# The shared expert of the last twelve tiles moved behind the last routed slot

## What is computed

```python
def step(carry, kvq):                     # first layer, token by token
    W, b = carry
    k, v, q = kvq                         # K, V, Q = x @ theta.T
    g = 2.0 / d_h * (W @ k + b - v)
    W = W - LR * jnp.outer(g, k)
    b = b - LR * g
    return ((W, b), W @ q + b)
x = _layernorm(x + attn(x))
# second layer: E = 8 experts of 512 -> 256 -> 512, the best K = 2 of each token
shared = silu(X @ sW1 + sb1) @ sW2 + sb2
activation = jnp.sqrt(softplus(X @ routing_W.T + expert_bias))
combine = weights of the top 2 of activation, 0 elsewhere
hdn = silu(einsum('nd,edh->enh', Xf, rW1) + rb1[:, None, :])
y = einsum('enh,ehd->end', hdn, rW2) + rb2[:, None, :]
x = _layernorm(x + shared + einsum('ne,end->nd', combine, y))
```

## Time and profile before

| | |
|---|---|
| median of 3 runs | 2472.6 us (2462.72 to 2474.06) |
| the profiled execution | 2472.85 us, its span 2471.0 us |
| busy, share of the span | PE 91%, PE weight loads 78%, DVE 61%, ACT 36%, POOL 46% |
| mean granted TensorE clock | 0.965 of full speed |
| chain that ended last | PE 77%, DVE 8%, unknown queue 5%, issue 4%, ACT 3%, DMA 2% |

### The profile page before, as it was taken

The page is one execution under the profiler, slowest core; times in us unless marked ns, Lnnn a source line. Parts: engine busy times, 40 slices in busy tenths (PEclk is TensorE's granted clock), DMA queues, the critical chain, the costliest instruction groups (busy, mean ns, idle before and its releaser), DMA issues.

```text
span 2471.0 us, 40051 instructions
## 1 busy us (share of the span) xinstructions
PE 2249.5 (91%) x13026; PEld 1939.6 (78%) x13026; DVE 1517.3 (61%) x3626; ACT 896.5 (36%) x1951; POOL 1147.9 (46%) x1090
## 2 busy tenths in 40 slices
PE   6999999999999999999999999888588888999980
PEld 5888888888888888888888888777477767888770
DVE  5556655566656776555666666546445334788797
ACT  3333333333333333333333333223444334444440
POOL 1234433344333337544455433753455555567674
PEclk9999999999999999999999999999789999999995
DMA  4111111111111111111111111102533334788798
GB/s 159 35 35 44 43 35 43 43 35 44 43 39 48 35 36 43 43 40 48 35 43 38 41 39 48 35 18 94 183 99 125 116 100 162 249 293 289 250 348 279
DMA packets 101143, 233.29 MB, mean 94 GB/s; under 512 B 18128, under 2 KB 18768, under 8 KB 100176
## 3 DMA queue, kind: packets, MB, share of 16 engines
q1 hardware_dynamic: 72720, 152.48, 18.0%
q0 software_dynamic: 27936, 78.21, 9.8%
q10 hardware_dynamic: 288, 0.04, 0.0%
HBM read 141.22 MB, written 89.53 MB: 93 GB/s over the span
## 4 chain that ended last, share of the span: by engine, by line
PE 77%; DVE 8%; another core or an unknown queue 5%; issue 4%; ACT 3%; DMA 2%; POOL 1%; DVEq 1%; ACTq 0%; SPq 0%; POOLq 0%
PE banks L115 22%; PE banks L117 22%; PE banks L116 21%; PE banks L121 6%; PE banks L713 2%; PE banks L456 1%; PE banks L552 1%; DVE b_small L1624 1%; PE banks L494 1%; DVE b_Y L1071 1%; DVE xc L1071 1%; PE banks L735 1%; DVE W L1068 1%; DVE b_XL L1068 1%
## 5 line engine op out<-in xcount | busy, mean ns | idle before, releaser
L115 PE MATMUL banks<-W 128*128 128x512 f32 (+1 forms) x2040 | 753.4, 369 | 23.1 <-DVE W L1068 20.1
L117 PE MATMUL banks<-W 128*128 128x512 f32 (+1 forms) x2040 | 719.2, 353 | 0.0
L116 PE MATMUL banks<-W 128*128 128x512 f32 (+1 forms) x2040 | 716.9, 351 | 0.0
L115 PEld LDWEIGHTS banks<-W 128*128 128x128 f32 x2040 | 388.7, 191 | 71.8 <-DVE W L1068 10.8
L117 PEld LDWEIGHTS banks<-W 128*128 128x128 f32 x2040 | 387.8, 190 | 55.1
L116 PEld LDWEIGHTS banks<-W 128*128 128x128 f32 x2040 | 389.3, 191 | 46.8
L776 ACT ACTIVATE W<-banks 128x512 fp32r<-128x512 f32 x320 | 191.1, 597 | 523.4 <-DVE banks L1068 226.3
L1674 POOL TENSOR_TENSOR W<-S,W 128x512 fp32r<-128x512 f32 x256 | 327.5, 1306 | 110.9 <-ACT W L776 110.8
L1674 POOL TENSOR_TENSOR X<-X,B 128x1024 f32<-128x1024 f32 x32 | 78.8, 2461 | 602.1 <-DMA X<-in_x 602.1
L776 ACT ACTIVATE W<-S 128x512 fp32r<-128x512 f32 (+1 forms) x288 | 179.8, 650 | 213.0 <-DVE S L1068 200.0
L1810 POOL DMA_INDIRECT ys<-b_Y,IDX x149 | 152.6, 1024 | 136.0 <-DVE b_Y L1068 111.9
(11 more groups left out here) (156 smaller groups left out, 4421.0 us busy)
## 6 DMA issues: line engine op xcount, KB each, us to landing
RG<-ys SPq DMA_DIRECT2D x128, 256.0 KB
XT<-in_xT SPq DMA_DIRECT2D x32, 512.0 KB
X<-in_x SPq DMA_DIRECT2D x32, 512.0 KB, 3.5
x1d<-X SPq DMA_DIRECT2D x64, 256.0 KB
zd<-X SPq DMA_DIRECT2D x64, 256.0 KB, 2.0
b_Y<-zd SPq DMA_DIRECT2D x64, 256.0 KB
out<-b_Y SPq DMA_DIRECT2D x64, 256.0 KB
S<-in_we SPq DMA_DIRECT2D x32, 256.0 KB, 4.8
```

Source lines behind the costliest of these rows:

```text
L115: e.matmul(o, ll, rh, start=start, stop=False, skip_group_check=True)
L116: e.matmul(o, lh, rl, start=False, stop=False, skip_group_check=True)
L117: return e.matmul(o, lh, rh, start=False, stop=stop, skip_group_check=True)
```

## The change

For the last group (tiles 52 to 63, `k.late` = 52) the first stage keeps only the routing logits: `up_x1` multiplies 8 columns, and `back_x1`, `down_x1`, `half_x1`, `residual_x1` and `store_z` return at once on every engine. `load_x` no longer waits for z there. While the last group's later slots run (from the 13th on, a slot can't be of expert 0) the shared expert's four blocks of weights are loaded again into spare Y buffers (iterations 131, 134, 137 and 140, SP), and split by ACT two and by POOL three iterations later into the place of expert 0. Twelve further items run in the slots' pipeline behind slot 148 (M = N + 12): they load a whole tile of `x1d` by SP instead of a gather, use static addresses, and their `down_late` adds the product onto the tile's Y buffer, into which POOL's new `residual` has put tile plus bias. The bases of the finals stay. The last finals' `scale` goes from DVE to ACT, for which POOL's `root` gets two more small operations. The scratch `zd` keeps 52 tiles.

```diff
 def plan_of(k):
-    seq = slots(a) + spread(slots(b), ends(a), 5) + spread(slots(c), ends(b), 5) + ends(c)
+    seq = slots(a) + spread(slots(b), ends(a), 5) + spread(slots(c), ends(b), 5)
+    p.again, p.stage = c["slot"] + c["tiles"], {}
...
+            if (i - p.again) % 3 == 1 and 0 <= i - p.again < 12:
+                q = (i - p.again) // 3
+                x = min(range(RING), key=lambda x: free[x])
+                free[x], p.stage[i] = i + 6, q
...
+    for j, (kind, n, g) in enumerate(ends(c)):
+        base = max(N + j + 1, base + 1)
+        p.finals.append(Final(n, g, base))
...
+    p.M = N + c["tiles"]
 # tensor_program
         for dc in range(KC):
-            z = mm3(e, o[:, 0:LGW], ..., dc == 0, dc == KC - 1)
+            z = mm3(e, o[:, c], ..., dc == 0, dc == KC - 1)   # c = H:LGW for i >= k.late
 def back_x1 / down_x1 (each engine), half_x1, residual_x1, store_z
+        if i >= k.late:
+            return
 def up(i)
+        else:
+            w.wait_ge(k.s_shlo, 7)
...
+                wh, wl = (k.W[:, j * 1024 + dc * H:j * 1024 + (dc + 1) * H] for j in range(2))
-    for i in range(-2, N + 2):
+    for i in range(-2, M + 2):
 # scalar_program
+    def split_again(q):
+        hi, _, raw = again(k, q)
+        w.wait_ge(k.d_sh, 48 + 16 * (q + 1))
+        w.wait_ge(k.s_dn, k.plan.again)
+        copy(hi, raw).then_inc(k.s_shhi, 1)
+    def scale(c):
+        y, i = k.Y[k.plan.buffer["final", c]], c % 2
+        w.wait_ge(k.s_crs, 2 * c + 2 + 2 * (c - k.plan.late + 1))
+        w.wait_ge(k.s_o, c)
+        e.activation(y[:], y[:], ACT.Identity, bias=k.sd2[:, i, 0:1], scale=k.sd2[:, i, 1:2]).then_inc(k.s_o, 1)
 # vector_program
+    def down_late(i):
+        y = k.Y[k.plan.buffer["final", k.plan.late + i - N]]
+        w.wait_ge(k.s_pre, i - N + 1)
+        w.wait_ge(k.s_dn, i + 1)
+        tt(y[:], at["dn", i], y[:], ALU.add).then_inc(k.s_Y, 1)
...
-        if i - 4 in k.plan.base:
+        if k.plan.base.get(i - 4, k.plan.late) < k.plan.late:
             scale(k.plan.base[i - 4])
 # gpsimd_program, load(i) for i >= 3
-            w.wait_ge(k.s_dn1, k.NTL)
+            w.wait_ge(k.s_dn1, k.late)
+            w.wait_ge(k.s_LG, k.NTL)
 # root(c), for c >= late
+            e.tensor_scalar(k.sd2[:, i, 0:1], k.mv2[:, i, 0:1], -1.0, None, ALU.mult).then_inc(k.s_crs, 1)
+            tt(k.sd2[:, i, 0:1], k.sd2[:, i, 0:1], k.sd2[:, i, 1:2], ALU.mult).then_inc(k.s_crs, 1)
+    def residual(i):
+        use = "final", k.plan.late + i - N
+        w.wait_ge(*k.d_tx.of(i - N))
+        w.wait_ge(k.d_sh, 144)
+        tt(k.Y[k.plan.buffer[use]][:], k.XN[i % XNS][:], k.brow[:, 0:D], ALU.add).then_inc(k.s_pre, 1)
+    def split_again(q):
+        tt(lo, raw, f32(hi), ALU.subtract).then_inc(k.s_shlo, 1)
 # sync_program, load_x(t)
-        w.wait_ge(*k.d_z.of(2 * t - 2))
-        w.wait_ge(*k.d_z.of(2 * t - 1))
+        if 2 * t <= k.late:
+            w.wait_ge(*k.d_z.of(2 * t - 2))
+            w.wait_ge(*k.d_z.of(2 * t - 1))
...
+    def load_again(q):
+        e.dma_start(again(k, q)[2], a["we"][E][:, q * D:(q + 1) * D]).then_inc(k.d_sh, 16)
+    def biases_again():
+        e.dma_start(k.brow[:, 0:D], a["b2"][:, E * D:(E + 1) * D].broadcast_to([P, D])).then_inc(k.d_sh, 16)
+        e.dma_start(k.b1T[:, 0:2], a["b1T"][:, 2 * E:2 * E + 2]).then_inc(k.d_sh, 16)
+    def load_late(i):
+        w.wait_ge(k.s_tp, i - XNS + 1)
+        w.wait_ge(k.s_pre, i - XNS - N + 1)
+        e.dma_start(k.XN[i % XNS][:], k.x1d[n * P:(n + 1) * P, :]).then_inc(k.d_tx.sem(i - N), 16)
```

More of the change, by code:

```diff
@@ L384, in plan_of @@
         p.buffer[use], p.before[use], holder[x] = x, holder.get(x), use
-    p.N = len(k.items)
+    p.N = N = len(k.items)
+    p.late = len(p.finals)
+    for j, (kind, n, g) in enumerate(ends(c)):
+        base = max(N + j + 1, base + 1)
+        use = ("final", len(p.finals))
+        p.finals.append(Final(n, g, base))
+        x = min(range(RING), key=lambda x: free[x])
+        assert free[x] <= N + j
+        free[x] = base + 6
+        p.buffer[use], p.before[use], holder[x] = x, holder.get(x), use
+    p.M = N + c["tiles"]
+    assert sorted(p.stage.values()) == list(range(4))
     p.base = {f.base: c for c, f in enumerate(p.finals)}
@@ L403, in free_of @@
     if old is None:
-        return [k.d_z.of(k.NTL - 2), k.d_z.of(k.NTL - 1)] if k.plan.buffer[use] < 6 else [(k.s_dn1, k.NTL)]
+        done = [(k.s_dn1, k.late), (k.s_LG, k.NTL)]
+        return done + [(k.s_X1T, k.NTL), (k.s_res, k.late), k.d_x1.of(k.NTL - 2), k.d_x1.of(k.NTL - 1)] if k.plan.buffer[use] < 6 else done
+    if old[0] == "stage":
+        return [(k.s_shlo, 4 + old[1])]
     return [k.d_out.of(old[1]) if old[0] == "final" else k.d_y.of(old[1])]
@@ L716, in up @@
     def up(i):
-        g = k.items[i]
         o = bank(w, ("up", i), k.s_HF, i + 1)
@@ L743, in down @@
             x = slice(c * P, (c + 1) * P)
-            wh, wl = (k.W[:, bass.ds(r * WC + 2048 + j * 1024 + c * D, D)] for j in range(2))
+            if i < N:
+                wh, wl = (k.W[:, bass.ds(regs[i] * WC + 2048 + j * 1024 + c * D, D)] for j in range(2))
+            else:
+                wh, wl = (k.W[:, 2048 + j * 1024 + c * D:2048 + j * 1024 + (c + 1) * D] for j in range(2))
             z = mm3(e, o, (hi[:, x], lo[:, x]), (wh, wl), c == 0, c == 1)
@@ L1009, in back @@
             o = at["hb", i][:, c * P:(c + 1) * P]
-            z = e.activation(o, o, ACT.Silu, bias=k.b1T[:, bass.ds(x * 2 + c, 1)])
+            b = k.b1T[:, bass.ds(x * 2 + c, 1)] if i < N else k.b1T[:, c:c + 1]
+            z = e.activation(o, o, ACT.Silu, bias=b)
         z.then_inc(k.s_HS, 1)
@@ L1194, in logits @@
         w.wait_ge(k.s_LG, i + 1)
-        w.wait_ge(k.s_HF1, i + 1)
+        if i < k.late:
+            w.wait_ge(k.s_HF1, i + 1)
+        else:
+            w.wait_ge(k.s_LG, i + 1)
         if g["x"]:
@@ L1650, in vector_program @@
             tick()
-        if 0 <= i < N:
+        if 0 <= i < M:
             back(i)
@@ L1840, in gpsimd_program @@
             scatter(*k.plan.scatter[i])
+        if i - 3 in k.plan.stage:
+            split_again(k.plan.stage[i - 3])
+        if N <= i < M:
+            residual(i)
 def sync_program(k, e):
@@ L1931, in sync_program @@
         load_weights(k, e, w, m)
-    N = k.plan.N
+    N, M = k.plan.N, k.plan.M
+    def load_again(q):
+        for x, v in free_of(k, ("stage", q)):
+            w.wait_ge(x, v)
+        w.wait_ge(k.s_shhi, 3 + q)
+        e.dma_start(again(k, q)[2], a["we"][E][:, q * D:(q + 1) * D]).then_inc(k.d_sh, 16)
+    def biases_again():
+        w.wait_ge(k.s_shhi, 7)
+        w.wait_ge(k.s_Y, k.plan.again)
+        e.dma_start(k.brow[:, 0:D], a["b2"][:, E * D:(E + 1) * D].broadcast_to([P, D])).then_inc(k.d_sh, 16)
+        w.wait_ge(k.s_HS, k.plan.again)
+        e.dma_start(k.b1T[:, 0:2], a["b1T"][:, 2 * E:2 * E + 2]).then_inc(k.d_sh, 16)
+    def load_late(i):
+        n = k.plan.finals[k.plan.late + i - N].n
+        for s, v in k.d_x1.last(k.NTL):
+            w.wait_ge(s, v)
+        w.wait_ge(k.s_tp, i - XNS + 1)
+        w.wait_ge(k.s_pre, i - XNS - N + 1)
+        w.wait_ge(*k.d_tx.of(i - N - 2))
+        e.dma_start(k.XN[i % XNS][:], k.x1d[n * P:(n + 1) * P, :]).then_inc(k.d_tx.sem(i - N), 16)
     def fetch(c):
@@ L1963, in sync_program @@
     for i in range(k.plan.end):
+        if N <= i + 4 < M:
+            load_late(i + 4)
         if i in k.plan.base:
-            fetch(k.plan.base[i])
+            if k.plan.base[i] < k.plan.late:
+                fetch(k.plan.base[i])
             rows(k.plan.base[i])
+        if i in k.plan.stage:
+            load_again(k.plan.stage[i])
+        if i == k.plan.again + 14:
+            biases_again()
         if i - 5 in k.plan.base:
             store_out(k.plan.base[i - 5])
-    for d in (k.d_out.last(k.NTL), k.d_x1.last(k.NTL), k.d_z.last(k.NTL), k.d_y.last(k.n_slots)):
+    for d in (k.d_out.last(k.NTL), k.d_x1.last(k.NTL), k.d_z.last(k.late), k.d_y.last(k.n_slots)):
         for s, v in d:
```

75 lines of the change are left out of this document (52 added, 23 removed).

## The result

| | before | after |
|---|---|---|
| median of 20 runs each | 2469.88 us (2461.96 to 2475.25) | 2460.61 us (2453.49 to 2471.54) |
| ratio | | 0.9966, 95% interval 0.9956 to 0.9976 |
| the profiled execution, its span | 2472.85, 2471.0 us | 2458.43, 2456.6 us |
| mean granted TensorE clock | 0.965 | 0.974 |

The changed kernel is 8.4 us faster (5.9 to 10.9); 9.8 were predicted. On a second chip it was 0.9973 (0.9955 to 0.9990). So the shares are read at marks, in two pairs of traces; a minus says earlier than before. A final is counted by its number, 52 being the first late one. The mean clock is higher after because PE now has work at the end: behind final 33 the granted clock was 0.76 before (PE idles there) and 0.95 after, and up to final 33 it was 0.98 in both.

What follows compares the result with a forecast made beforehand. PE was taken to bound the first stage, DVE the slots with finals, POOL and DMA close. From the profiled 2472.85 us, 21.0 gained in front and 11.2 lost behind gave 2463.0 us, range 2450 to 2480.

Steps and rivals of the forecast that it cites:

- front: First stage through the boundary to the first up of the slots: 21.0 us gained (9.6 to 28.8).
- back: Weight reload and everything behind the last slot: 11.2 us lost (4.2 to 31).
- rounds of 3.8 us: Sign of being wrong: intervals between late mixes of 3.8 us, where 4.1 us were predicted.
- Steps 27 to 30: First-stage steps with the fill of tiles 52 to 59: 2.25 us saved a step, 9.0 in all (5.6 to 12.3).
- Step 31: Last first-stage step, bound by a chain: earlier x and less shared work in the inverse save 8.0 us (3 to 10).
- The boundary's end: Between first stage and slots: 0.5 us (0 to 2) to the first gather, 3.5 (1 to 4.5) at first up.
- The rival in which the boundary eats step 31's gain: Weight blocks and 2 MB of biases set the boundary; step 31's gain and the 0.5 go: 2471.6 us, 22%.
- The reload: Iterations 131 to 143, shared expert's weights loaded and split again: 1.5 us lost (0 to 5).
- The first late mix: Behind the last slot: added turns, one back and a residual before the last send move it 3.2 us (2.4 to 5).
- The rounds: Eleven intervals from first to last late mix: POOL sets 4.1 us each, 42.7 against 36.14, 6.5 us lost.
- the first rival: Back hidden better: POOL's operations short, DVE sets the pace, reload free; 5 us lost, 2456.8 us, 22%.
- The third rival: POOL bounds the tail: residual and DVE's mixes take turns, rounds of 5.7 us; 2483.4 us, 8%.

Runs made afterwards that it cites:

- both cures: Changed kernel with reloaded weights' low parts on DVE and staging in expert 0's bias row; three kernels had both, each with another edit: 0.9969, 0.9961, 0.9976.
- scale from 48 on: Changed kernel with scale of finals 48 to 51 also on ACT: 2339.04 us, ratio 0.9995.

## Why the prediction was right, and where its terms were off

The mechanism was right in the large: a front worth 21 us, a back that takes a good half of it again. The time was 2460.6 against 2463.0 us, and that it came so near is in part luck. By the marks, 21 us less the back's 14.2 to 16.5 leave 4 to 7 us, and 8.4 (5.9 to 10.9) were measured. The back cost 3 to 5 us more than said, and stretches that nobody edited vary by more than that between executions. And one of the prediction's own signs of being wrong was there: rounds of 3.8 us.

**Steps 27 to 30, predicted 9.0.** From tile 52's turn to tile 60's: 235.2 to 225.3 us, 10.0 (9.3 in the second pair). The sum is right, its parts are not. `up` saved 0.2 and not 0.7: a matmul of 8 columns took 0.11 us, and not the 0.065 taken over from two transposes. The two `down_x1` left 0.94 and 0.86, as step 0 said. The X1l wait held the first part, as said. Two waits went that I hadn't read. In step 28 PE had stood 1.50 us for a bank, released by DVE's RG (start 1523.91); with fewer users of the banks it is gone. In step 27 it was a wait of 0.95 us for ACT's MM (start 1471.36). By steps the gain was 2.8, 3.8, 3.5 and -0.2. Only steps 27 and 28 show what the edit is worth. Steps 29 and 30 took 58.6 to 65.6 us in all traces of the chips with before at 2460 to 2471, with idle time of PE that nothing in the kernel releases (6.67 us at once in step 30 before, 5.36 after) and a granted clock of 0.5 (1.2 GHz) for 7 to 14 us in each; on the fast chip, with the same changed front, they took 50.4. The prediction had read its step at 1380 to 1432 us, where neither shows. So the sum of 10.0 for 9.0 is partly luck as well.

**Step 31, predicted 8.0:** 6.7 and 7.8 us. Right; of the 2.8 for the late x 1.3 to 2.3 are real. `u_part` came 14.8 us earlier and not 17.

**The boundary's end, predicted 0.5 and 3.5:** from tile 62's turn to the first slot's turn 2.5 and 0.9, from there to the first `up` 2.8 and 2.9. The rival in which the boundary eats step 31's gain is out.

**The reload, predicted 1.5 with an upper end of 5:** 7.7 and 9.6 us in the two pairs. This is the term that failed, above its upper end. I had asked what POOL's splits delay on POOL, and not what they do to the operation of DVE beside them; and I had counted the DMA bytes, but not that SP would stand for buffers which the ring had given up with nothing to spare (10.5 us in three waits). With both cures together it was 1.4 to 4.2. The sign named for it, DVE waiting for a root, did not come.

**The first late mix, predicted 3.2 (2.4 to 5):** 3.5 and 4.4 from `stats` 46 on. The turns are in it as said; two residuals beside a scale (1.0 and 1.4 us) are not in my sum.

**The rounds, predicted 6.5 (from 1.8):** 3.1 and 2.7. The first interval was 4.26 for 4.24. The full ones were DVE's, as the first rival had it, and 3.78 instead of POOL's 4.1. The two small operations took 0.25 and 0.20 us and not 0.4 each, and the residual lay beside DVE operations that read `banks`, which neither slows. POOL's bound came only in the three rounds without a turn but with a residual.

The third rival had the residual hold up the mixes. It did so in part: in after three mixes took 1.94 us for 1.52, 1.3 us in all, and with scale from 48 on two took 3.03 and 3.05. But it did not set the full rounds.

The Trainium skill ("SBUF — State Buffer", who interferes with whom) also lists `tensor_scalar` among the operations that can enter a mode that uses both ports, where their operands allow it, so the rule can cover `scale` (0.54 to 1.91 us here), which I had left out; I had weighed only the mix. By the same page of the Trainium skill (the section on SBUF's two sides) whoever starts first gets the pair. In the rows here POOL's operation kept its 1.3 us each time, and DVE's, even where its recorded start was 0.3 us earlier (2324.91 against 2325.23), paid. The earlier trace rows show the other case: POOL's longest bias add, 1.73 us for 1.29, started at 1737.45 beside a split of DVE with two inputs in SBUF that had started 0.7 us earlier. So it is not always DVE that pays.

## What to carry to other kernels

Work moved to another engine has two prices: its time there, and what it does to the neighbour that runs beside it. Look in the trace for which operation of the other engine will lie there; here POOL's operation of 1.3 us cost DVE nothing beside one that read PSUM, and 1.0 to 1.4 us beside a `scale`. A ring of buffers with none to spare turns an extra user into a wait of the queue that issues everything behind it. Where one engine is freed by 2 us, look first for the queue that stands at that place: SP's wait of 5.3 to 6.5 us for the last send was there in every kernel, and it came to light in each version that made DVE earlier. And read a step's price from the very steps that change: two of the four here ran 9 to 14 us longer than the one that was read.
